# The mixture of experts of blocks 0 and 1 moved beside the attention of blocks 2 and 3

## What is computed

```
x = layernorm(x + L0_attn(x));  x = layernorm(x + L0_ffn(x))       # first layer: unchanged
# L1 attention: 16 heads of 16, causal over all 2048 tokens
qkv = x @ w_qkv.T;  scores = q @ k.T / 4, masked causally;  probs = softmax(scores)
x = layernorm(x + (probs @ v) @ w_o.T)
# L1 mixture: 32 experts of inner width 96, top 8 cut where the running share passes 0.8
logits = x @ gate_weight.T; combine = renormalised kept weights, [tokens, 32]
for each expert e: out += (silu(x @ Wg_e.T) * (x @ Wu_e.T)) @ Wd_e.T * combine[:, e]
x = layernorm(x + out)
```

## Time and profile before

| | us |
|---|---|
| median of 3 runs | 1611.99 |
| lowest, highest | 1581.69, 1615.75 |
| the profiled execution | 1600.74 |
| its span | 1599.0 |

### The profile page before, as it was taken

The page is one execution under the profiler, slowest core; times in us unless marked ns, Lnnn a source line. Parts: engine busy times, 40 slices in busy tenths (PEclk is TensorE's granted clock), DMA queues, the critical chain, the costliest instruction groups (busy, mean ns, idle before and its releaser), DMA issues.

```text
span 1599.0 us, 20300 instructions
## 1 busy us (share of the span) xinstructions
PE 1464.6 (92%) x7956; PEld 1043.3 (65%) x7956; DVE 936.7 (59%) x1777; ACT 627.5 (39%) x884; POOL 262.4 (16%) x343
## 2 busy tenths in 40 slices
PE   6689999999999889999999999888889999999995
PEld 5578778788788655344443443454478888888885
DVE  3555753754745457678758878763345545575445
ACT  3032322422322212466546656545523444444331
POOL 3220110200200001012111211301011222232221
PEclk9699999999999865699869999977889999999998
DMA  6000000000000438002400600000001111111110
GB/s 267 0 1 1 1 1 1 0 1 1 20 1 27 149 119 117 1 2 35 46 2 5 77 2 1 21 10 1 1 21 40 45 45 50 50 41 50 50 57 27
DMA packets 31831, 55.41 MB, mean 35 GB/s; under 512 B 6392, under 2 KB 13304, under 8 KB 31224
## 3 DMA queue, kind: packets, MB, share of 16 engines
q1 hardware_dynamic: 29688, 53.85, 13.6%
q0 software_dynamic: 2048, 0.27, 0.2%
HBM read 43.21 MB, written 10.49 MB: 34 GB/s over the span
## 4 chain that ended last, share of the span: by engine, by line
PE 79%; DVE 14%; ACT 4%; issue 3%; POOL 0%; DMA 0%; POOLq 0%; DVEq 0%; ACTq 0%
PE ps L1449 50%; PE ps L1647 9%; PE ps L1717 9%; PE ps L1695 4%; DVE mpart L1236 4%; PE ps L1666 1%; DVE x L1039 1%; PE ps L1471 1%; PE ps L1456 1%; PE ps L1502 1%; ACT probs L940 1%; PE ps L1487 1%; PE ps L1726 1%; PE ps L1513 1%; DVE mpart L1246 1%
## 5 line engine op out<-in xcount | busy, mean ns | idle before, releaser
L940 ACT ACTIVATE probs<-ps 128x1024 f32<-128x1024 f32 (+3 forms) x320 | 277.6, 896 | 238.2 <-PE ps L1695 237.2
L1449 PE MATMUL ps<-xtd,gu 128*128 128x512 f32 x1152 | 283.5, 401 | 7.8 <-DVE x L1279 4.8
L1236 DVE TENSOR_REDUCE mpart<-ps 128x1 f32<-128x512 f32 x384 | 238.0, 682 | 49.8 <-PE ps L1647 49.6
L1647 PE MATMUL ps<-stack 48*128 48x512 f32 (+3 forms) x832 | 232.9, 425 | 36.3 <-DVE mpart L1236 21.0
L1449 PEld LDWEIGHTS ps<-xtd,gu 128*128 128x128 f32 x1152 | 216.3, 191 | 58.8 <-issue 9.8
L1647 PEld LDWEIGHTS ps<-stack 48*128 48x128 f32 x832 | 129.2, 213 | 180.4 <-DVE mpart L1236 110.2
L1449 PE MATMUL ps<-ma,b 128*128 128x512 f32 x672 | 169.0, 401 | 10.3 <-DVE x2f L1185 7.4
L1695 PE MATMUL ps<-stack 50*128 50x512 f32 (+3 forms) x640 | 171.0, 449 | 5.5 <-ACT probs L940 5.4
L1717 PE MATMUL ps<-probs,vaug 128*32 128x512 f32 (+3 forms) x1280 | 172.8, 617 | 1.9 <-POOL probs L820 1.6
L1449 PEld LDWEIGHTS ps<-ma,b 128*128 128x128 f32 x672 | 126.9, 191 | 44.1 <-DVE x2f L1185 10.7
L1449 PEld LDWEIGHTS ps<-dn,hpart 128*128 128x128 f32 x1152 | 144.3, 189 | 5.3 <-DVE hpart L1020 1.0
(11 more groups left out here) (175 smaller groups left out, 1676.9 us busy)
## 6 DMA issues: line engine op xcount, KB each, us to landing
gu_raw<-in_wgu SPq DMA_DIRECT2D x48, 256.0 KB, 2.6
stack<-qk_dram SPq DMA_DIRECT2D x72, 128.0 KB, 9.1
qk_dram<-qk_out SPq DMA_DIRECT2D x16, 512.0 KB, 2.9
dn_raw<-in_wdn SPq DMA_DIRECT2D x48, 128.0 KB, 2.7
stack<-qk_dram SPq DMA_DIRECT2D x48, 64.0 KB, 2.4
x<-in_x_tm SPq DMA_DIRECT2D x4, 512.0 KB, 5.1
xt_in<-in_x_fm SPq DMA_DIRECT2D x1, 2048.0 KB, 8.4
out<-x SPq DMA_DIRECT2D x4, 512.0 KB, 3.1
```

The source lines that it names most:

```text
L940: act.activation(probs[:, (2 * r + p) % 4, :, off:BLK], banks(bank)[:, :, off:BLK], ACT.Exp, scale=float(HD) ** -0.5).then_inc(exp_done.se ...
L1236: ins = dve.tensor_reduce(part[:, p, qt % TPB, 2 + kb:3 + kb], ps[:, bank, :], AX_X, ALU.max)
L1449: mm = pe.matmul(out, lhs(i), rhs(k), start=first and n == 1, stop=last and n == todo, **more)
L1647: return pe.matmul(out, stack[lo:lo + KROWS, g % 2, 0, b, p, P * t:P * (t + 1)], stack[lo:lo + KROWS, g % 2, 1, kb, p, k0:k0 + width], sta ...
```

## The change

The greedy walk is gone. In its place stands ORDER, a string of 1411 letters, one for each piece of work, which is spelled out into the plan.

- Rounds come in eight visits: first (g, 0) and (g, 1) for g from 0 to 3, then (g, 2) and (g, 3). So blocks 0 and 1 have left the attention after 48 of 160 steps.
- `stack` becomes `keys` and `queries`, two slots each, loaded by visit: two or four blocks of keys and two of queries. Load v waits for the last scores of visit v - 2.
- The mixture of blocks 0 and 1 is done a block at a time, in 48 single passes: `gate` and `up` one after the other in bank 7, `split` and `low` for the parts, `down` into banks 2 and 3. Each has half the products of a pass for two blocks. They stand in the list from behind step 96 on. From the first gate on units have two banks (4, 5), and from the first down on scores have one pair (0, 1).
- The mixture of blocks 2 and 3 stays as 24 passes for two blocks, behind the list. So weights are fetched and split 72 times, not 48.
- Scores may be three steps ahead of values.

The core of the diff:

```
-    steps = [(g, qb, kt) for g in range(NG) for qb in range(NB) for kt in range(TPB * (qb + 1))]
-    rounds = [(g, qb) for g in range(NG) for qb in range(NB)]
+    visits = [(half, g) for half in range(2) for g in range(NG)]
+    rounds = [(g, 2 * half + i) for half, g in visits for i in range(2)]
+    steps = [(g, qb, kt) for g, qb in rounds for kt in range(TPB * (qb + 1))]
+ORDER = ( "qTqLRqVTqWNuuuquuuquwuuVwuuuMTwVuuuuqqVXuuuSSuuSuSuSuPuuuSSuSuPuu...
...
+     "uSPuSuSPuuSXSPuuSPuuSuSuPuuSSPuuSUuuSPiSSulPuuSSPuuSGuuSPuuSSuPuuSSPuuSUuuSSPiSSulPuuSPDwuuDwuuGuuUuuGiuuOluPu"
...
+    "lSPUSDiwGlSPUSDiwGlSPUSDiwGlSPUSDiwGlDwUPGiOlUaDiwGlbUDwGicdlUeDilrwGsDwUfGiklUmDiwGlUxDiwGlDwUilDAw" )
+    # u unit, S scores of a pair, P values, M maxima, O sums, G gate, U up, D down, i split, l low, w weights, X load
+    for letter in "".join(ORDER):
+        if letter == "q": plan.append(("qk", bm[n], pair()))
+        elif letter == "u": plan.append(("unit", units[n], one()))
+        elif letter == "S": plan.append(("st", (n // HP, n % HP), pair()))
+        elif letter == "D":
+            if n == 0: wide, taken["pair"] = wide[:1], 0
+            plan.append(("down", n, 2))
...
+            def gate_alone(n, bank):                      # PE
+                pe.wait_ge(*wd_lo.after(n))
+                bank_free(pe, "gate", n)
+                gate_or_up(n, 0, bank).then_inc(gate_ps.sem, 1)      # six products of 512 columns
+            def up_alone(n, bank):
+                bank_free(pe, "up", n)
+                gate_or_up(n, 1, bank).then_inc(up_ps.sem, 1)
+            def down_alone(n, bank):
+                pe.wait_ge(*h_part_lo.after(n))           # twelve products of 256 columns
...
+            def hidden_alone(n, bank):                    # DVE
+                dve.wait_ge(*gated.after(n)); dve.wait_ge(*up_ps.after(n)); dve.wait_ge(*h_part_lo.after(n - 1))
+                hmul1 = ps[bank] * silu1;  hmul1 = hmul1 * ce0[block]
+            def load_visit(v):                            # SP
+                for which, into, b0, b1 in ((1, keys[v % 2], 0, 2 + 2 * half), (0, queries[v % 2], 2 * half, 2 * half + 2)):
...
+                elif kind == "load":
+                    sp_.wait_ge(*st_ready.after((last_step[2 * (key - 2) + 1], HP - 1)))
+                    load_visit(key)
```

More of the change, by code:

```diff
@@ L68, in attention_plan @@
-        mine += [("full", g, qt, kb, p, a) for qt in range(TPB * qb, TPB * (qb + 1)) for kb in range(qb) for p in range(HP)
-                 for a in range(2)]
-        units += mine
-        closes[mine[-1]] = n
-    plan, count = [], {"pair": 0, "one": 0}
-    ones, hand = (4, 5, 7), 0.12
-    now = {"pe": 0.0, "dve": 0.0, "act": 0.0}
-    mode = [None]
-    free = {b: 0.0 for b in range(8)}
-    def mark(kind, key):
-        plan.append((kind, key, None))
-    def pair(kind, key, bank=None):
-        if bank is None:
-            bank = 2 * (count["pair"] % 2)
-            count["pair"] += 1
-        plan.append((kind, key, bank))
-        return bank
@@ L88, in one @@
-    def one(kind, key):
-        bank = ones[count["one"] % 3]
-        for queue, act in ((to_copy, copy_maxima), (to_head, head)):
-            if queue and queue[0][2] == bank:
-                act()
-        count["one"] += 1
-        plan.append((kind, key, bank))
-        return bank
-    def next_one():
-        return free[ones[count["one"] % 3]]
-    def next_pair():
-        return free[2 * (count["pair"] % 2)]
-    def on_pe(start, cost, kind):
-        now["pe"] = max(now["pe"], start) + cost + (0.11 if kind != mode[0] else 0.0)
-        mode[0] = kind
@@ L290, in attention_plan @@
-    assert not todo and not at_step, (len(todo), at_step)
-    end = len(rounds) - 1
-    while to_head:
-        head()
-    move = [i for i, e in enumerate(plan) if e[:2] in (("pv", len(steps) - 1), ("ucopy", end), ("out", end), ("head", end))]
-    kept = {plan[i][0]: plan[i] for i in move}
-    for i in reversed(move):
-        del plan[i]
-    if ("out", end) not in [e[:2] for e in kept.values()]:
-        kept["out"] = ("out", end, ones[count["one"] % 3])
-    pair("gu", (0, 0, 0), 2)
-    mark("pv", len(steps) - 1)
@@ new lines, in attention_plan @@
+    bm = [(b, m) for b in range(NB) for m in range(2)]
+    chain = {"a": "turnO", "b": "proj", "c": "normC", "d": "turnD", "e": "logit", "r": "rexp", "s": "best", "f": "share",
+             "k": "kept", "m": "combine", "x": "ce", "V": "v", "T": "turnC", "G": "gate", "U": "up", "i": "split", "l": "low",
+             "A": "acc", "n": "statD", "z": "normD", "w": "whi", "X": "load"}
+    once = {"L": "lora", "R": "resB", "N": "normB", "W": "raws", "y": "wo", "Y": "wg1"}
+    plan, count, taken, turned, left = [], collections.Counter(), collections.Counter(), [], []
@@ new lines, in attention_plan @@
+    assert count["S"] == HP * len(steps) and count["u"] == len(units) and count["O"] == len(rounds)
+    assert count["D"] == 2 * JT and count["A"] == 2 and count["n"] == count["z"] == 1 and count["x"] == 2 and count["X"] == len(visits) - 1
+    weights = count["w"]
+    for j in range(JT):
+        for tb in range(2):
+            plan.append(("gu", (j, tb), 4 + 2 * tb))
+        if j == 2:
+            plan.append(("statD", 1, None))
+        elif j == 3:
+            plan.append(("normD", 1, None))
+        if j:
+            plan.append(("down2", j - 1, None if j > 1 else 0))
+            if weights < 3 * JT:
+                plan.append(("whi", weights, None))
+                weights += 1
@@ L507, in build @@
         mix_read = sig("mix_read", range(NT))
-        blocks = [(st, b) for st in "ABCD" for b in range(NB)]
+        rounds, steps, units, closes, plan = attention_plan()
+        blocks = [(st, b) for st in "AB" for b in range(NB)]
+        blocks += [({"resC": "C", "statD": "D"}[kind], key) for kind, key, bank in plan if kind in ("resC", "statD")]
+        blocks += [("D", b) for b in range(2, NB)]
         var_ready = sig("var_ready", blocks)
```

667 lines of the change are left out of this document (297 added, 370 removed).

## The result

The changed kernel takes 1680.5 us (median of four runs, 1676.2 to 1688.0), the kernel before 1598.8 beside it (four runs, 1581.7 to 1615.8): 1.058 times as long, 95% interval 1.049 to 1.067. The profiled execution took 1680.9 us, its span 1679.1. The forecast was 1535 us.

What follows compares the result with a forecast made beforehand. PE alone was taken to bound the last mixture, no single engine the attention, where hand-overs lose PE time. Terms 505 + 83 + 394 - 15 + 345 + 205 + 16 = 1533 us, kept as 1535; range 1460 to 1620.

Steps and rivals of the forecast that it cites:

- The clock: Steps 1 to 112: 28 us for the low clock, kept from the kernel before; range 0 to 67 us.
- A: Stretch from 505 us to the end of step 112; forecast 83 + 394 - 15 = 462 us.
- slower: Low clock from the prologue stays until full-height products come near step 96: 106 us, 1639 us in all; chance 0.10.
- Three steps ahead: Steps 1 to 112: DVE could go from 79% to about 90% busy; taken as -15 us (0 to -40).
- The loads: Loads between visits, steps 1 to 112: each may hold PE some microseconds; taken at 0, range 0 to 26 us.
- Units and tails: Before the first step 31 us less; behind it 13 us for 19 more units, 30 for two blocks' tails and routing.
- Two of the signs that I had named: Wrong by: clock in 590 to 800; PE waiting on loads ahead of visits 2 to 4; PE waiting for silu or multiply.
- ACT needs 4.3 us and PE about 6: Loop that fills the end of ORDER: time per value step, pass and two pairs on each engine.
- eaten by waits: Silu or multiply queued behind others holds gate and up's bank, 48 us, or loads and clock: 1575 to 1620; chance 0.22.
- B: Steps 113 to 160 with the 48 single passes: 338 us of PE work and 7 us of waits, 345 us.
- The gain of lying beside: Last 48 steps, with passes beside them: 138 us of attention become 345 - 202 = 143.
- First values: Stage from 505 to the first value products: 83 us, not 114, so near 588 and not 619.

Runs made afterwards that it cites:

- experiment 10: Changed kernel with Exp for Silu in the single passes, scores at most two steps ahead, loads of visits 2 and 3 issued early: 1602.9 us, ratio 0.997.
- experiment 12: Changed kernel with the mixture of blocks 0 and 1 behind the attention, scores two ahead, loads of visits 2 and 3 early: 1772.2 us, ratio 1.112.

## Why the prediction was wrong

**To step 112: 462 forecast, 553 measured.** This is the larger miss, and three terms of the sum failed.

The clock. I wrote that I couldn't derive this term, kept 28 us of the kernel before, and allowed 67 at most for the first 48 steps. Measured are 310 us at the low level against 150. A us at half clock does about half the work (eight value products take 1.86 us there and 1.00 at full clock), so by this estimate the extra 160 us cost 80, and A is 83 us longer than before. The rival *slower*, at 0.10, had the sign and about the size: a low clock in the first 96 steps, for 106 us. Its cause, the missing full-height products, is neither shown nor excluded: one filler of 512 columns a step raised the clock by 0.04 to 0.07 and gave no time, one of 128 columns didn't raise it; but the last 48 steps have 0.59 alone and 0.97 with the mixture's products among them. Against it I had set 62 steps of the kernel before near full clock; those had a lead of two.

"Three steps ahead", taken as -15 us (0 to -40). Its sign was wrong. With the walk's new interleaving it costs the kernel before 7%, 98 us in A, and taking it out of the changed kernel gives 16. I argued from DVE at 79% that more scores in hand would fill it, to 90%; DVE is busy 299 of the 488 us from 570 to 1058, 61%. `probs` still holds two steps, so the third score makes ACT's head wait for values.

The loads, taken at 0 with 0 to 26 us in the range. Without two of them 19 us go. The estimate went by bytes (1.5 MB at 124 GB/s, 13 us); the trace of before had 72 issues on one queue, 22 of them in this row, 0.64 us each:

```profile
599.88 13.97 SPq L695 DMA_DIRECT2D stack<-qk_dram  x22
```

The issues, 11 us for load 2 and 14.7 for load 4, are the longer part of a load.

Units and tails in A can't be told apart from the rest. The forecast had 31 us less ahead of the first step and 13 + 30 us more behind it, 12 more in all; length times clock has 3 more (398 against 395), so no large miss hides there.

Two of the signs that I had named stand in this stretch: the clock in 590 to 800 is 0.65, before 0.78, and PE waits for a load ahead of the first unit of visits 2, 3 and 4.

**Steps 113 to 160 with the passes: 345 forecast, 401 measured.** The failed step is "ACT needs 4.3 us and PE about 6". ACT needs 4.3 + 2 x 1.28 = 6.9 us of the 7.45 measured. The rows of the kernel before showed silu and exponential as neighbours nowhere, and I didn't ask what the neighbourhood costs; its trace had 13 table loads of 1283 ns, and I read none of them. The Trainium skill says it, page ScalarE: Activation LUTs, sections What ACT_TABLE_LOAD costs and Table sets: the hidden batching unit: a change between sets of functions costs a load of about 1283 ns, and calls should be batched by set. The trace agrees to the nanosecond with the load. The page adds some 1380 ns for draining; here the loads stand without a gap behind the silu and ahead of the exponential (1342.33, 1342.35 to 1343.63, 1343.64), so no such second half shows. That tanh shares exp's table is on the same page, and the run with Tanh has no loads between them.

The rival *eaten by waits* had 48 us for this stretch, near the 56 measured, but from silu and multiply holding the one bank without any table loads. In experiment 10 PE waits 2.5 us for silu and 3.7 for the multiply in all of B, so the nearness is luck.

With the loads out B is 363 us against 345, at PE busy 347 against my 338 of PE work: the PE part of that term was right within 3%, and the waits are 16 us where I allowed 7. POOL's 49 us more were right, and hidden: among PE's waits in B there is none for POOL.

**The gain of lying beside.** I took 138 us for the last 48 steps alone. Alone they take 218 (experiment 12), at a clock of 0.59, and single passes alone 5.7 us each and not 4.2. So the move itself gains more than I had it gain, 131 us, but the comparison that counts is with the old order and its paired passes: steps 113 to 160 and 48 single passes of the new kernel (401) against 608 - 203 = 405 us before. The work is nearly the same; before, the tails of blocks 0 and 1 and a routing lie in it, which the new order has in A. That is 4 us where the forecast had 405 - 345 = 60. Without the table loads it is 42.

**The other terms.** First values at 588: four steps at 570, the rest from 602 on, on either side of it. Paired passes 205, measured 203; end 16, measured 17. With all three causes out the kernel takes 505 + 514 + 363 + 203 + 17 = 1602, and what is left against the 1533 of the sum is 52 us in A, at a clock of 0.76, and 18 in B.

**What stays open.** What sets the clock in A. A lead of three goes with a lower one (0.69 against 0.84 in the kernel before, 0.72 against 0.74 in the changed one), the last 48 steps without a mixture beside them sink to 0.59 with a lead of two as well, and a PE without a gap can stay at the low level for 20 us and more. In the new order nothing brought the mean in A above 0.77 except fillers, which cost what they gave. That the product of length and clock stays the same shows that the clock goes with the loss; that the clock is its cause and not its companion is argued from the windows in which PE is full at half clock, and not shown by a run that changes the clock alone. In the kernel before no run kept the interleaving and changed the lead alone, and none added full-height products in the amount that the mixture has. Load 4 issued early wasn't tried.

## What to carry to other kernels

Where a change brings two functions of ACT next to each other that stood apart, count their alternations and look whether they share a table before anything else; and if the cure gives the bank to another reader, count how long the bank is now held. Before more work is put in flight, look at the buffer behind it: where that stays as it was, the queue's head waits for a slot, and here the kernel with the longer lead was 7% slower. When the mean granted clock of a stretch is below one, multiply it by the length: if two versions agree in the product, the loss goes with the clock, and adding up idle times won't account for it. What lowers the clock may still be a hand-over, and is found by taking edits out one at a time.

## What the runs showed of the hardware

- A table load between silu and exponential takes 1283 ns on ACT, with no visible gap around it; exponential and tanh alternate without one.
- Issuing one DMA of 64 KB takes SP's queue 0.42 us and 0.04 to the next; one of 128 KB takes more, twelve 9.02 us against 5.72. On ACT's queue eleven of 64 KB take 5.19 us, in which ACT runs nothing.
- TensorE was granted 1.2 GHz in windows in which it was busy for 20.00 of 20 us (680 to 700 in the kernel before with a lead of three), and 2.4 GHz in windows with 1.4 us of gaps. The last 48 steps of the attention alone had a mean of 0.59, beside 128-row products of the mixture 0.97.
- Over 16 kernels without added products in that stretch the granted cycles of nearly the same work agreed within 5% (383 to 402 us at full clock), the time by 24% (470 to 585).
- A 128x512 multiply took 1294 ns on POOL against 704 on DVE, and moving it gained nothing.
